# A state-space layer between two expert layers: a two-phase convolution for the first batch, and a router with wide products between its narrow ones

## The chip, the cores and the metric

The kernel is one program on one core of a Trainium2 chip. The core has a matrix engine (TensorE, PE in the rows; its weight loads are PEld), VectorE (DVE), ScalarE (ACT), GpSimd (POOL) and SyncE (SP), which here only issues transfers. The engines run side by side and wait for one another on semaphores. The metric is the device time of one execution in microseconds (us). Three runs of the kernel before took 1475.5, 1475.68 and 1467.76 us, median 1475.5.

## The reference

The input x has 8 batches of 512 tokens of 256 numbers. Four layers follow one another, each added to x after a layer norm of its input:

```
x = x + attention(layernorm(x))      # linear attention, 16 heads
x = x + experts(layernorm(x))        # softmax router, best of 8 experts, 256 -> 512 -> 256
x = x + state_space(layernorm(x))    # below
x = x + experts(layernorm(x))        # the same weights again
```

The state-space layer projects each token to 512 channels, runs a full convolution over 4 successive tokens (512 channels in, 512 out) and adds a bias; call the result u. From u come the step dt = clip(sigmoid(u W + b)), and two vectors B and C of 16 numbers for every token. Then for each of 512 channels and 16 states a linear recurrence runs over the 512 tokens, `state = exp(dt * A) * state + dt * B * u + 1e-6`, and y is the sum of the states times C, plus D * u; y is gated by silu(z) and projected back to 256. Everything is float32.

## The kernel before, in words

All of x stays on the chip (32 tiles of 128 tokens). The stages are written one after another, each engine's program in an order written out by hand; no planner orders anything.

**Attention** (0 to about 196 us) and, grown into its end, the **first router**. `x_turn` (L1300 through `turned`) transposes a batch of x, ScalarE copies it, and `logits` (L1419) multiplies it with the router's weights, which are only 8 columns wide. VectorE then computes the routing in one chain of small steps (`feed`, L999 to L1059). TensorE helps it twice: with two products by a triangle and by ones (L1464, L1466), and with four groups of 8 products of 80 columns (L1475) that turn the places of the tokens into lists. VectorE prepares the next group while TensorE works on the last. The semaphore `f_lg` lets the first pair start, `f_hot` each group.

**The folded taps.** Projection and convolution are both linear, so the kernel multiplies them first: 4 taps times 2 halves give 8 products, each of four 128x512 matmuls (`tap`, L1449), copied by ScalarE to `tapw` (`tap_copy`, L618). Their inputs are `ipw` (the projection) and `cw` (one tap of the convolution, 1 MB), which SyncE loads at L369 and L373 after the rows of x and their scales have been stored. Products 0 to 3 of the eight are made during the first router, as work for TensorE between the steps of the chain; products 4 to 7 follow the expert layer.

**The expert layer** (239 to 393 us) gathers 39 tiles of tokens in the order of their experts and is bound by TensorE (L1504, L1513). Its result goes to memory and comes back into x by 8 loads (L382).

**The first batch of the state-space layer** (407 to 472 us) is prepared in the open, since no recurrence runs yet. VectorE takes the statistics of the layer norm (L839, for tiles 4 to 31 in one piece, then its scales). ScalarE normalises (`m_norm`, L686), TensorE transposes (`m_turn`), ScalarE copies (`m_xtcopy`, L693). `m_conv` (L1567) makes each 128 channels of u (four outputs `o`) with 8 matmuls of 512 columns: 4 taps times 2 halves of the input. ScalarE adds the bias (`m_uevac`, L699). `m_uturn` (L1575) turns u, `m_bcmm` (L1584) gives B and C, `m_dtmm` (L1598) the input of dt, again four outputs of four matmuls. ScalarE takes tanh (`m_thevac`, L718), VectorE clips (`m_clip`, L1121), TensorE turns dt (`m_dturn`, L1613), VectorE multiplies dt and u (`m_weigh`, L1134), and ScalarE multiplies by B for the first state (`m_input`, L755, four tiles). `m_spread` (L1300) turns that product into PSUM, and the first recurrence (`m_scan`, L1197) can run. ScalarE has also to make the exponentials (`m_decay`, L745) and to normalise batch 1.

**The loop** (472 to about 1260 us) has 64 slots for each of 8 batches, one recurrence in each. In every slot ScalarE makes one exponential and one tile of input, TensorE turns one tile and does the preparation of the next batch by a table of slots (`CONV_AT` and so on), GpSimd multiplies by C. The router and the expert layer of the end follow (to 1469 us); there TensorE has products by ones between its groups (`spin`, L1455), whose result nobody reads.

## Time and profile before

| | |
|---|---|
| three runs | 1475.5, 1475.68, 1467.76 us |
| the profiled execution | 1471.08 us, its span 1469.3 us |
| busy: TensorE, VectorE, ScalarE, GpSimd | 1366.5, 1011.8, 937.7, 861.1 us |
| mean granted TensorE clock | 0.978 |
| the chain that ended last | TensorE 67%, ScalarE 16%, VectorE 10% |

The span runs from the first instruction to the last; 1.8 us of the execution lie around it. The chain of waits goes back from the last instruction to whatever released each step, so it tells which engine a stretch waits for. Granted clock is 1.00 for 2.4 GHz and 0.50 for 1.2 GHz. TensorE does a float32 product in two passes, each with a record of its own: "x16" of L1567 in the rows is 8 matmuls of the code. A transpose has one record.

### The profile page before, as it was taken

Reading aid. Unit: us, or ns where it says so; the run is one execution under the profiler, and the core shown is the slowest. Engines: PE = TensorE matmul, PEld = TensorE weight load, DVE = VectorE, ACT = ScalarE, POOL = GpSimd, SP = SyncE. Lnnn points to the kernel's source line nnn. Section 1 sums busy time; section 2 is a strip of 40 time slices with the busy share of each in tenths; the row PEclk is TensorE's granted clock in tenths of the full one; section 3 lists DMA queues with packets and bytes.
Section 4 is the critical chain, followed back from the end, with each engine's and each line's share of the span. In section 5 each row is a group of like instructions: output and inputs, shape, how many; then the busy total and the mean of one; then the engine's idle time right before and its main releaser. Section 6 shows DMA issues by size and latency. Waiting matters only on the chain.

```text
span 1469.3 us, 22230 instructions
## 1 busy us (share of the span) xinstructions
PE 1366.5 (93%) x7040; PEld 949.6 (65%) x7040; DVE 1011.8 (69%) x1529; ACT 937.7 (64%) x1737; POOL 861.1 (59%) x436
## 2 busy tenths in 40 slices
PE   5899998999998999999999999999999887979997
PEld 2566686999744555565655655655656576569996
DVE  6666634333332899899899898998998988853332
ACT  1222231344314999899999998999999999214442
POOL 1111002555200899798898897998988979225552
PEclk9999989999998999999999999999999979999999
DMA  9200044777420598898997997988979979376662
GB/s 301 85 29 29 19 98 144 211 206 210 153 65 16 118 219 195 179 221 186 201 222 181 205 220 176 218 190 193 223 170 204 230 195 234 79 235 203 208 210 82
DMA packets 108229, 248.39 MB, mean 169 GB/s; under 512 B 19097, under 2 KB 49950, under 8 KB 94048
## 3 DMA queue, kind: packets, MB, share of 16 engines
q0 software_dynamic: 23104, 131.96, 41.5%
q1 hardware_dynamic: 82944, 113.68, 25.6%
q10 hardware_dynamic: 2080, 1.47, 0.3%
q8 instruction: 55, 0.90, 0.2%
q14 instruction: 46, 0.38, 0.1%
HBM read 116.72 MB, written 18.94 MB: 92 GB/s over the span
## 4 chain that ended last, share of the span: by engine, by line
PE 67%; ACT 16%; DVE 10%; issue 4%; DMA 1%; another core or an unknown queue 1%; SPq 0%; DVEq 0%; ACTq 0%; POOLq 0%; POOL 0%
PE ps L1300 11%; PE ps L1513 9%; PE ps L1504 9%; PE ps L1567 7%; ACT arena L745 7%; PE ps L1598 7%; ACT arena L755 7%; PE ps L1325 4%; PE ps L1640 3%; PE ps L1629 3%; DVE arena L1197 3%; PE ps L1362 2%; PE ps L1584 2%; PE ps L1316 2%; PE ps L1449 1%
## 5 line engine op out<-in xcount | busy, mean ns | idle before, releaser
L500 POOL TENSOR_TENSOR arena<-arena 128x2048 f32<-128x2048 f32 x91 | 425.1, 4684 | 118.6 <-DVE arena L1197 117.4
L1300 PEld LDWEIGHTS ps<-cst,arena 128*128 128x128 f32 x2428 | 295.3, 143 | 280.1 <-issue 187.7
L1197 DVE TENSOR_TENSOR_SCAN arena<-arena,ps 128x512 f32<-128x512 f32 x364 | 431.7, 1209 | 62.3 <-PE ps L1300 58.7
L1300 PE MATMUL ps<-cst,arena 128*128 128x128 f32 x2428 | 365.7, 278 | 51.2 <-ACT arena L755 24.3
L745 ACT ACTIVATE arena<-arena,a_neg 128x512 f32<-128x512 f32 x512 | 365.9, 715 | 43.3 <-DVE arena L1197 29.6
L755 ACT ACTIVATE arena<-arena,m_bt 128x512 f32<-128x512 f32 x512 | 362.9, 709 | 3.8 <-DVE arena L1134 2.2
L1567 PE MATMUL ps<-arena,tapw 128*128 128x512 f32 x512 | 255.1, 600 | 0.7 <-ACT arena L693 0.7
L1197 DVE TENSOR_TENSOR_SCAN x<-arena,ps 128x512 f32<-128x512 f32 x148 | 175.7, 1209 | 21.9 <-PE ps L1300 20.6
L500 POOL TENSOR_TENSOR x<-x,arena 128x2048 f32<-128x2048 f32 x36 | 169.8, 4728 | 14.7 <-DVE x L1197 12.7
L1078 DVE TENSOR_TENSOR arena<-ps,arena 128x256 f32<-128x256 f32 x78 | 33.1, 425 | 205.7 <-PE ps L1513 131.4
L456 POOL DMA_INDIRECT arena<-rows,arena x78 | 75.9, 973 | 158.1 <-DVE arena L1058 134.9
L1504 PEld LDWEIGHTS ps<-arena 128*128 128x128 f32 x1248 | 154.7, 196 | 3.8
L1504 PE MATMUL ps<-arena 128*128 128x128 f32 x1248 | 154.9, 279 | 0.0
L1513 PE MATMUL ps<-arena 128*128 x624 | 147.5, 380 | 3.3 <-ACT arena L644 3.3
L637 ACT ACTIVATE arena<-ps 128x256 f32<-128x256 f32 x78 | 30.0, 385 | 157.8 <-PE ps L1300 156.5
L1598 PE MATMUL ps<-arena,dtw 128*128 128x512 f32 x256 | 128.6, 597 | 0.6 <-ACT arena L699 0.6
L1513 PEld LDWEIGHTS ps<-arena 128*128 128x128 f32 x624 | 112.5, 190 | 16.0 <-issue 3.7
L644 ACT ACTIVATE arena<-ps,b1t 128x128 f32<-128x128 f32 x312 | 89.3, 370 | 43.8 <-issue 29.5
L1567 PEld LDWEIGHTS ps<-arena,tapw 128*128 128x128 f32 x512 | 85.1, 193 | 36.1 <-issue 33.7
L447 POOL TENSOR_TENSOR x<-x,arena 128x1024 f32 (+1 forms) x8 | 18.9, 2358 | 120.0 <-DVE arena L868 114.4
L471 POOL DMA_INDIRECT residual<-arena x39 | 39.4, 1011 | 68.4 <-DVE arena L1085 67.2
L471 POOL DMA_INDIRECT out_x<-arena x39 | 39.3, 1008 | 67.5 <-DVE arena L1085 67.5
(164 smaller groups left out, 1573.0 us busy)
## 6 DMA issues: line engine op xcount, KB each, us to landing
arena<-arena POOLq DMA_DIRECT2D x52, 1024.0 KB, 8.3
arena<-in_W SPq DMA_DIRECT2D x94, 512.0 KB, 8.2
arena<-c_rows SPq DMA_DIRECT2D x128, 256.0 KB, 3.7
arena<-x POOLq DMA_DIRECT2D x28, 1024.0 KB, 8.4
x<-arena POOLq DMA_DIRECT2D x24, 1024.0 KB, 8.3
rows<-x SPq DMA_DIRECT2D x16, 512.0 KB, 4.2
x<-residual SPq DMA_DIRECT2D x12, 512.0 KB, 5.9
x<-in_x SPq DMA_DIRECT2D x8, 512.0 KB, 11.2
```

The source lines that it names most:

```text
L456: g.indirect_dma_start(out=t_x[j % XB], out_offset=None, in_=xs[r], in_offset=bass.IndirectOffsetOnAxis(ap=idx[:, j:j + 1], axis=0))\
L471: g.indirect_dma_start(out=x_mid if r == 0 else T["out"].rearrange("b s d -> (b s) d"), out_offset=bass.IndirectOffsetOnAxis(ap=idx[:, j:j ...
L500: g.tensor_tensor(h, h, m_c[i % RC].unsqueeze(1).to_broadcast([P, KI, SEQ]), ALU.mult)\
L644: last = a.activation(t_ht[par][:, k, :], ps[4 + par][:, k * P:(k + 1) * P], ACT.Relu, bias=b1t[:, row(e), k:k + 1].rearrange("p a b -> p ...
L745: a.activation(m_a[g % RA], m_dt[b % 2][:, k, :], ACT.Exp, scale=a_neg[:, k, n:n + 1])\
L755: a.activation(m_dbt[i % 2][:, c, :], m_wt[b % 2][:, c, :], ACT.Copy, bias=1e-6, scale=m_bt[b % 2][:, c, n:n + 1]).then_inc(S("m_dbt"), 1)
L1197: v.tensor_tensor_scan(out=h[:, k, :], data0=m_a[g % RA], data1=ps[SCAN_BANK[g % 3]][:, :], initial=0.0, op0=ALU.mult, op1=ALU.add).then_i ...
L1300: return t.transpose(bank, src[:, k * P:(k + 1) * P], ident)
L1504: last = t.matmul(ps[4 + par][:, h * P:(h + 1) * P], t_w1[j % WR][:, k, h * P:(h + 1) * P], t_xt[par][:, k, :], start=(k == 0), stop=(k == ...
L1513: last = t.matmul(ps[6 + par][:, 0:D], t_ht[par][:, k, :], w2[:, row(e), k, :].rearrange("p a h -> p (a h)"), start=(k == 0), stop=(k == K ...
L1567: mm = t.matmul(ps[CONV_BANK[o]][:, :], tapw[:, k, d, o * P:(o + 1) * P], m_xt[n % 2][:, d, k:k + SEQ], start=(i == 0), stop=(i == TAPS * ...
L1598: mm = t.matmul(dt_bank(n, o)[:, :], dtw[:, k, o * P:(o + 1) * P], m_u[n % 2][:, k, :], start=(k == 0), stop=(k == KI - 1))
```

## The change

In the **router**: SyncE loads `ipw` and the first two taps at the start of the program, behind the other weights, and not after the stores. The four matmuls of product 0 are made one by one in rounds 3 to 6 of the loop over `x_turn` and `logits`; product 1 takes the place that product 0 had, product 2 that of products 1 and 2, and the four matmuls of product 3 stand one behind each group of L1475. Other banks hold the results.

In the **first batch**: u is split into odd and even tokens. With a0 to a3 the taps and x the input, both phases share the sums (a3 + a2) and (a1 + a0) times the even tokens of x, 4 matmuls of 256 columns (`both_bank`). Each phase then adds 4 matmuls of 256 (or 255) columns by single taps and differences of neighbouring tokens. GpSimd makes the two sums of taps (`tap_sum`, 1024 elements a lane each) and the two differences (`xd_first`, 512 elements a lane each). ScalarE copies the shared part with the bias into the odd places of u (`m_both`), and VectorE adds it to both phases (`m_join`), which takes the place of `m_uevac`. VectorE's statistics are cut so that each join falls between two pieces. In the **last steps** `m_dturn` of output 1 goes between the matmuls of output 3, those of 2 and 3 to both sides of the first half of batch 1's transposes; VectorE clips before it weighs; ScalarE normalises batch 1 earlier and makes only two of the four tiles of the first input, VectorE the other two. The other batches are as before. Some semaphores are shared by both routers (`f_n`, `f_yb`).

```diff
@@ -32,6 +32,9 @@
 PAD = TAPS - 1
+HALF = SEQ // 2
+TURN_OF = ((0, 0), (0, 1), (1, 1), (1, 0))
+PARTS, BOTH_END = 3 * len(TURN_OF), len(TURN_OF) - 1
 LN_EPS, NORM_EPS = 1e-5, 1e-6
...
@@ -85,6 +88,9 @@
+TAP_BANK = (7, 1, 0, 1, 0, 1, 0, 1)
...
@@ -269,6 +276,12 @@
                 for c in (RING * CPB, (RING + 2) * CPB)]
+        def first_h(j):
+            return m_h[j].rearrange("p k t -> p (k t)")
+        xd_first = first_h(0)[:, 0:2 * KD * HALF].rearrange("p (s k t) -> p s k t", s=2, k=KD)
+        tap_sum = first_h(1).rearrange("p (j k n) -> p j k n", j=2, k=KD)
         m_c = [s.take(SEQ) for _ in range(RC)]
...
@@ -335,6 +354,15 @@
+            def send_tap(k):
+                if k >= 2:
+                    sp.wait_ge(S("tap_mm"), KD * (k - 1))
+                sp.dma_start(cw[k % 2], T["conv"][k].rearrange("(k p) d -> p k d", p=P)).then_inc(S(f"ld_cw{k}"), 16)
+            sp.dma_start(ipw, T["ip_x"].rearrange("(k p) d -> p k d", p=P)).then_inc(S("ld_cw0"), 16)
+            send_tap(0)
+            send_tap(1)
@@ -366,14 +394,7 @@
             sp.wait_ge(S("row_zeroed"), 32)
-            sp.dma_start(ipw, T["ip_x"].rearrange("(k p) d -> p k d", p=P)).then_inc(S("ld_cw0"), 16)
-            def send_tap(k):
-                if k >= 2:
-                    sp.wait_ge(S("tap_mm"), KD * (k - 1))
-                sp.dma_start(cw[k % 2], T["conv"][k].rearrange("(k p) d -> p k d", p=P)).then_inc(S(f"ld_cw{k}"), 16)
-            for k in range(TAPS - 1):
-                send_tap(k)
+            send_tap(2)
             send_w1(0)
@@ -481,6 +502,15 @@
+            for j in (1, 0):
+                g.wait_ge(S("tapw"), KD * (TAPS - 2 * j))
+                g.tensor_tensor(tap_sum[:, j], tapw[:, TAPS - 1 - 2 * j], tapw[:, TAPS - 2 - 2 * j], ALU.add)\
+                    .then_inc(S("m_zero"), 1)
+            g.wait_ge(S("m_xtc"), KD)
+            for s in range(2):
+                g.tensor_tensor(xd_first[:, s], m_xt[0][:, :, PAD + 1 - 2 * s:PAD + SEQ - 2 * s:2],
+                                m_xt[0][:, :, PAD:PAD + SEQ - 1:2], ALU.subtract).then_inc(S("m_xd"), 1)
@@ -615,7 +645,7 @@
                 a.wait_ge(S("tap_mm"), n + 1)
-                a.activation(tapw[:, n // KD, n % KD, :], ps[n % 2][:, :], ACT.Copy).then_inc(S("tapw"), 1)
+                a.activation(tapw[:, n // KD, n % KD, :], ps[TAP_BANK[n]][:, :], ACT.Copy).then_inc(S("tapw"), 1)
@@ -699,6 +729,12 @@
+            def m_both(o):
+                a.wait_ge(S("m_bothmm"), o + 1)
+                a.activation(m_u[0][:, o, 1::2], both_bank[:, o % 2 * HALF:(o % 2 + 1) * HALF], ACT.Identity,
+                             bias=mvec[:, 0, o:o + 1]).then_inc(S("m_both"), 1)
@@ -778,22 +814,22 @@
                     m_utevac(0, o - 1)
-                m_uevac(0, o)
+                m_both(o)
             m_utevac(0, KI - 1)
             m_bchi(0)
-            for o in range(KI):
+            for o in range(KI - 1):
                 m_thevac(0, o)
-                if o == 2:
-                    for k in range(KD):
-                        m_decay(k)
+            for k in range(KD):
+                m_decay(k)
+            for c in range(XN):
+                m_norm(1, c)
+            m_thevac(0, KI - 1)
             for g in range(KD, AHEAD):
                 m_decay(g)
-            for c in range(XN):
-                m_norm(1, c)
-            for c in range(CPB):
-                m_input(0, c)
             for c in range(XN, CPB):
                 m_norm(1, c)
+            for c in range(CPB // 2):
+                m_input(0, c)
             for k in range(KD):
...
@@ -1103,18 +1139,26 @@
             v.wait_ge(S("ld_mid0"), 16)
-            def m_stats(lo, hi):
-                first_stats(lo, hi)
+            def shifts(lo, hi):
                 v.scalar_tensor_tensor(out=nw[2][:, lo:hi], in0=mean[:, lo:hi], scalar=-1.0, in1=rstd[:, lo:hi],
...
-            m_stats(0, CPB)
+            first_stats(0, CPB)
+            shifts(0, CPB)
...
+            def m_join(o):
+                v.wait_ge(S("m_both"), o + 1)
+                v.wait_ge(S("m_umm"), o + 1)
+                u = m_u[0][:, o, :].rearrange("p (t s) -> p t s", s=2)
+                v.tensor_tensor(u, ps[CONV_BANK[o]][:, :].rearrange("p (s t) -> p t s", s=2),
+                                u[:, :, 1].unsqueeze(2).to_broadcast([P, HALF, 2]), ALU.add).then_inc(S("m_u"), 1)
@@ -1264,9 +1308,31 @@
             v.wait_ge(S("ld_mid1"), 16 * (BATCH - 1))
-            m_stats(CPB, NCH)
-            for q in range(SLOTS):
-                m_pre(0, q)
+            for c in range(CPB, NCH // 2):
+                row_stats(c)
+            m_join(0)
+            for c in range(NCH // 2, NCH - 1):
+                row_stats(c)
+            link(row_stats(NCH - 1))
+            m_join(1)
+            layer_norm_scales(CPB, NCH)
+            shifts(CPB, NCH)
+            m_join(2)
+            m_join(3)
+            m_clip(0, 0)
+            m_clip(0, 1)
+            m_btcopy(0)
+            m_weigh(0, 0)
+            m_clip(0, 2)
+            m_weigh(0, 1)
+            m_weigh(0, 2)
+            m_clip(0, 3)
+            m_weigh(0, 3)
+            v.wait_ge(S("m_wt"), KI)
+            v.wait_ge(S("m_btc"), 1)
+            for c in range(CPB // 2, CPB):
+                v.tensor_scalar(m_dbt[0][:, c, :], m_wt[0][:, c, :], m_bt[0][:, c, 0:1], 1e-6, ALU.mult, ALU.add)\
+                    .then_inc(S("m_dbt0"), 1)
             binds = v.value_load(far_flag[0:1, 0:1], min_val=0, max_val=P * KI * NS)
@@ -1420,6 +1486,19 @@
+            def tap_part(n, c):
+                k, d = n // KD, n % KD
+                if c == 0:
+                    t.wait_ge(S(f"ld_cw{k}"), 16 if k else 32)
+                    if n == 0:
+                        t.wait_ge(S("a_xadd"), BATCH)
+                    if n >= 2:
+                        t.wait_ge(S("tapw"), n - 1)
+                mm = t.matmul(ps[TAP_BANK[n]][:, :], ipw[:, c, d * P:(d + 1) * P], cw[k % 2][:, c, :],
+                              start=(c == 0), stop=(c == KI - 1))
+                if c == KI - 1:
+                    mm.then_inc(S("tap_mm"), 1)
@@ -1438,17 +1517,13 @@
-            def tap(k, d):
-                t.wait_ge(S(f"ld_cw{k}"), 16 if k else 32)
-                n = KD * k + d
-                if n >= 2:
-                    t.wait_ge(S("tapw"), n - 1)
+                if 0 <= i - 3 < KI:
+                    tap_part(0, i - 3)
+            def tap(n):
                 for c in range(KI):
-                    last = t.matmul(ps[n % 2][:, :], ipw[:, c, d * P:(d + 1) * P], cw[k % 2][:, c, :],
-                                    start=(c == 0), stop=(c == KI - 1))
-                last.then_inc(S("tap_mm"), 1)
+                    tap_part(n, c)
@@ -1459,14 +1534,13 @@
                     t.wait_ge(S("f_raw"), BATCH - 1)
-                    tap(0, 0)
+                    tap(1)
                 t.wait_ge(S("f_lg"), 2 * r + 2)
...
                 if r == 0:
-                    for n in range(1, 3):
-                        tap(n // KD, n % KD)
+                    tap(2)
                 else:
@@ -1476,14 +1550,15 @@
                     last.then_inc(S("f_inv"), 1)
-                    if r and i < NCH // GROUP - 1:
+                    if r == 0:
+                        tap_part(3, i)
+                    elif i < NCH // GROUP - 1:
                         spin(1)
                 if r == 0:
-                    tap(1, 1)
                     t.wait_ge(S("tapw"), KD * 2)
                 def tr(par, n):
-                    t.wait_ge(S(f"f{r}_n{par}"), n + 1)
+                    t.wait_ge(S(f"f_n{par}"), tiles_done(r, par) + n + 1)
                     if not (isinstance(n, int) and n == 0):
...
@@ -1552,6 +1627,32 @@
+            def m_conv_first(o, i):
+                part, (d, j) = i // len(TURN_OF), TURN_OF[i % len(TURN_OF)]
+                first, last = i % len(TURN_OF) == 0, (i + 1) % len(TURN_OF) == 0
+                if o == 0 and i == 0:
+                    t.wait_ge(S("m_zero"), 4)
+                    t.wait_ge(S("m_xtc"), KD)
+                if o == 0 and part and first:
+                    t.wait_ge(S("m_xd"), part)
+                if o and i == 0:
+                    t.wait_ge(S("m_both"), o)
+                if o >= 2 and part == 1 and first:
+                    t.wait_ge(S("m_utc"), o - 1)
+                if part == 0:
+                    lo = o % 2 * HALF
+                    mm = t.matmul(both_bank[:, lo:lo + HALF], tap_sum[:, j, d, o * P:(o + 1) * P],
+                                  m_xt[0][:, d, PAD - 2 * j:PAD - 2 * j + SEQ - 1:2], start=first, stop=last)
+                else:
+                    lo = (2 - part) * HALF
+                    mm = t.matmul(ps[CONV_BANK[o]][:, lo + j:lo + HALF], tapw[:, TAPS - part - 2 * j, d, o * P:(o + 1) * P],
+                                  xd_first[:, part - 1, d, 0:HALF - j], start=first, stop=last)
+                if i == BOTH_END:
+                    mm.then_inc(S("m_bothmm"), 1)
+                if i == PARTS - 1:
+                    mm.then_inc(S("m_umm"), 1)
@@ -1646,7 +1747,9 @@
                 if k == 0:
-                    t.wait_ge(S("m_dbt"), g + CPB)
+                    t.wait_ge(S("m_dbt"), g + CPB - CPB // 2)
+                if g == 0:
+                    t.wait_ge(S("m_dbt0"), CPB // 2)
                 if g >= 3:
...
@@ -1723,9 +1826,9 @@
             for o in range(KI):
-                for i in range(TAPS * KD):
-                    m_conv(0, o, i)
-                    if o and i == TAPS:
+                for i in range(PARTS):
+                    m_conv_first(o, i)
+                    if o and i == PARTS // 2:
                         m_uturn(0, o - 1)
@@ -1741,9 +1844,13 @@
                 m_dtmm(0, 3, k)
-            for o in range(1, KI):
-                m_dturn(0, o)
-            for c in range(CPB):
+                if k == 1:
+                    m_dturn(0, 1)
+            m_dturn(0, 2)
+            for c in range(XN):
+                m_turn(1, c)
+            m_dturn(0, 3)
+            for c in range(XN, CPB):
                 m_turn(1, c)
```

## Rows read from the trace of the kernel before

**Rows 1.** Chain of waits, first router (start us, length us, what).

```profile
204.27 10.97 DMA arena<-in_conv
215.38 5.73 PE ps L1449 x8
```

**Rows 2.** Timeline of TensorE, first router (start, length, what, idle before).

```profile
205.37 1.85 PE L1419 MATMUL ps<-wr,arena 128*128 128x8 f32 x16
...
207.98 5.64 PE L1419 MATMUL ps<-wr,arena 128*128 128x8 f32 x32
```

**Rows 3.** Busy TensorE, weight loads, VectorE, ScalarE, GpSimd; granted clock, DMA share, GB/s: first router.

```profile
207.00:209.00 2.00, 2.00 (x20) 2.00 (x21) 0.00 (x0) 1.01 (x3) 0.00 (x0) 1.00 0.80 98
209.00:219.00 10.00, 8.25 (x29) 6.12 (x29) 4.07 (x10) 1.08 (x4) 0.00 (x0) 0.51 0.72 232
```

**Rows 4.** Timeline of VectorE, first router.

```profile
213.99 0.42 DVE L999 TENSOR_TENSOR arena<-arena,scales 128x256 f32<-128x256 f32 x1 [12.34 <-ACT arena L599]
...
217.07 0.60 DVE L1008 TENSOR_TENSOR arena<-arena 128x256 f32<-128x256 f32 x1
...
221.65 0.42 DVE L1016 TENSOR_REDUCE arena<-ps 128x8 f32<-128x256 f32 x1 [3.35 <-PE ps L1464]
...
237.62 0.20 DVE L1057 TENSOR_SCALAR arena<-ps 128x40 f32<-128x40 f32 x1 [0.96 <-PE ps L1475]
```

**Rows 5.** Timeline of VectorE, second router.

```profile
1286.71 0.59 DVE L1008 TENSOR_TENSOR arena<-arena 128x256 f32<-128x256 f32 x1
...
1288.16 0.42 DVE L1016 TENSOR_REDUCE arena<-ps 128x8 f32<-128x256 f32 x1 [0.23 <-PE ps L1464]
...
1304.77 0.20 DVE L1057 TENSOR_SCALAR arena<-ps 128x40 f32<-128x40 f32 x1 [1.66 <-PE ps L1475]
```

**Rows 6.** Timeline of SyncE's queue, 0 to 70 us.

```profile
38.84 0.43 SPq L336 DMA_DIRECT2D mvec<-in_mvec  x1
63.70 0.38 SPq L341 DMA_DIRECT2D rows<-x  x1
```

**Rows 7.** Chain of waits, first batch of the state-space layer.

```profile
410.96 12.96 PE ps L1567 x26
...
425.34 7.07 PE ps L1567 x16
...
442.30 2.77 PE ps L1567 x6
...
457.93 3.44 PE ps L1598 x8
...
463.19 0.67 PE ps L1613 x4
...
466.35 0.70 DVE arena L1134
...
467.08 2.56 ACT arena L755 x4
...
470.18 2.03 PE ps L1300 x8
```

**Rows 8.** Chain of waits, expert layer: 256 columns moving.

```profile
255.71 1.73 PE ps L1513 x8
```

**Rows 9.** Groups of VectorE in 195 to 260 us, shapes apart.

```profile
L1031 DVE TENSOR_REDUCE arena<-arena 128x32 f32<-128x256 f32 x1 | 0.6, 604 | 0.0
L1001 DVE TENSOR_REDUCE arena<-arena 128x32 f32<-128x256 f32 x1 | 0.4, 420 | 0.0
```

**Rows 10.** Groups of GpSimd, shapes apart.

```profile
L447 POOL TENSOR_TENSOR x<-x,arena 128x1024 f32 x7 | 16.5, 2356 | 114.4 <-DVE arena L868 114.4
```

**Rows 11.** Timeline of VectorE, first batch.

```profile
411.70 9.24 DVE L839 BATCH_NORM_STATS2 stats<-x 128x6 f32<-128x256 f32 x28 [3.40 <-DMA x<-residual]
```

**Rows 12.** Busy time by stretches, first batch, with granted clock (columns as in rows 3).

```profile
411.00:414.00 3.00, 3.00 (x4) 1.44 (x5) 2.29 (x7) 0.40 (x1) 0.00 (x0) 0.50 0.01 3
...
466.00:475.00 9.00, 5.99 (x21) 4.01 (x20) 1.91 (x2) 7.14 (x13) 0.00 (x0) 0.50 0.01 2
```

20 lines of the change are left out of this document (12 added, 8 removed).

## The prediction, made before the changed kernel was run

> **What bounds the kernel now.** I read the chain of waits first, then the timelines of each engine in the two stretches that the change touches, then the granted clock there. Everything between these stretches (attention, both expert layers, the loop of 64 slots a batch) is left alone by the diff, so its length should stay and only its start should move.
>
> In the first router the chain goes through a transfer and then through VectorE. SyncE begins to load the first tap at 204.27, behind the rows and the scales; it lands 10.97 us later and product 0 starts at 215.38 [rows 1]. Its four wide matmuls take 5.73 us there, because TensorE runs at 1.2 GHz: the granted clock is 1.00 to 209 and 0.51 from 209 to 219 [rows 3]. The second product by ones stands behind product 0, so VectorE, which had the one-hot table ready at 217.67, gets on only at 221.65 and has waited 3.35 us [rows 4]. From there VectorE needs 15.97 us to the list of tokens (L1057, 237.62), and the expert layer can start.
>
> In the first batch the chain is TensorE almost throughout: 16 records of 512 columns take 7.07 us, 0.442 each [rows 7]. The convolution ends at 445.07 (442.30 + 2.77); call that E. The matmuls of dt's last output start at E + 12.86 and take 3.44. Then comes a stretch in which each step waits for another engine: turns at 463.19, the last weighing at 466.35, four inputs by ScalarE from 467.08 (2.56 us), eight transposes from 470.18 that take 2.03 us at half clock; the first recurrence can start at 472.21, E + 27.14 [rows 7]. The clock is 0.50 from 466 to 475 [rows 12].
>
> **Convolution.** Removed: 4 outputs x 8 matmuls x 2 records x 0.442 = 28.3 us. Added: 4 x 12 x 2 records of 256 columns. The nearest row is the expert layer's product of 256 columns, 8 records in 1.73 us, 0.216 each [rows 8]: 20.8 us. That is -7.5. The unknown is the moving operand with a step of two in the shared part (16 of the 48 matmuls, 6.9 us); no row of TensorE shows one. VectorE reads with a step 0.604 us for what takes 0.420 without, 1.44 times [rows 9]; at that price the shared part costs 3.0 more. Below nothing is excluded, since the same columns pass. I take nothing, because the step is of two elements here and of 32 there, and keep +3.0 for the range. The Trainium skill (SBUF: State Buffer, Door 1: The DMA port swizzle) says that a line of 16 bytes with two hits is read at full rate; a step of two has two hits, so by it the term is nothing, and by the row +3.0.
>
> The start: GpSimd's first sum can run before the last tap is copied, the second takes 2.36 us [rows 10] from 407.7 and ends near 410.1, or 410.7 if it stands behind the first. TensorE has waited until 410.96 for the first copy of x and now waits for both copies: +0.5. The differences have half the elements, 1.2 us each, and are wanted 1.7 and 3.5 us later (at 2.4 GHz; later still at 1.2): hidden, and at twice the price 1.3 us would show. VectorE has 9.24 us of statistics from 411.70 [rows 11]; 12 tiles end at 415.7, join 0 is due near 418, the other 16 tiles need 5.3 us and end near 424, join 1 is due near 424.6, the scales (3.5 us) end near 429 and join 2 is due near 431. Each join (0.7, as the weighing [rows 7]) is wanted by the turn 7 matmuls or 3 us later, so a join a third slower for its steps still costs nothing. The copy of the shared part has the same cover. If the statistics came late, the turn would wait for the join. Half clock at the start: 411 to 414 costs 1.5 us now [rows 12] and should again. Sum: -7.0.
>
> **Last steps**, from the new E with all parts at full clock. Output 3 of dt: 12.86 + 3.44, and a turn of 0.45 between: 16.75. Turn of output 2: 17.2; weighing it: 17.9; clip 3 (tanh was ready at 17.5): 18.6; turn 3 (0.67): 19.3; weighing (0.70): 20.0; two inputs on ScalarE (half of 2.56): 21.3, while VectorE makes the other two, 1.2 to 1.4 together if they are as long as a pass from PSUM; four transposes (0.45): 21.8. Half of batch 1's transposes fall into the wait for clip 3, the rest behind turn 3, ending before 21.3. Against 27.14 that is -5.3. ScalarE's two normalisings moved ahead of tanh 3 use 1.1 us in which it would wait for TensorE; the new single queue order leaves tanh 3 free at 15.1, due at 16.75. At half clock the transposes take 0.85: -4.9.
>
> **Clock behind it.** Between 472.2 and 475.5 TensorE still runs at half clock on matmuls of batch 1, which are the chain: 1.6 us. The stretch without wide matmuls shrinks from 10.8 us (461.4 to 472.2) to 5.1. Between -1.6 and 0 I take -0.8.
>
> **Router.** The early loads (2.5 MB) follow at 39.3, and the queue is empty until 63.7 [rows 6]: nothing waits. Four wide matmuls now lie between the narrow products: +3.5 us on TensorE. If they keep the clock up, the last 32 narrow records take 3.4 instead of 5.64 (16 take 1.71 at full clock [rows 2]); the logits end 1.2 later and L999 runs at 215.2, not 213.99. The table is ready at 218.9; product 1 has ended at 218.3; in the second router L1016 follows 0.86 after the end of L1008 [rows 5], so it runs at 219.8, -1.9. Then the four groups with one wide matmul between: the second router has that pattern, 16.61 us from L1016 to L1057 against 15.97 [rows 4, 5], +0.6. Together L1057 at 236.4: -1.2. What was product 3 behind the groups (3.65 us) lay under the gathering and gives nothing. Product 2 alone ends near 223.3, the first group is due at 226.4: 3 us of idle TensorE that can cost the clock and up to 1.5 us. The term lies between -1.9 and +2.4 (below); I take -1.2.
>
> **Sum:** -7.0 - 5.3 - 0.8 - 1.2 = -14.3, against the profiled 1471.08: 1456.8. That execution lies 4.4 under the median of the three runs; the four have a mean of 1472.5, and 14.3 under that is 1458. I give **1458**.
>
> **Rivals.**
> 1. *The clock falls where I keep it.* A stretch of narrow products or transposes alone has cost it twice [rows 3, 12]. If the logits end at half clock, they end 2 us later still and product 1 takes 3.5 more, partly in the wait for the table: L1057 1.2 to 2.4 later than now. In the last steps half clock costs 0.4 and the 0.8 behind. Sum -10: 1462. For it: the wide matmuls stop at round 6, and the last 3.4 us before product 1 are narrow as before. Against: narrow products had run since attention's end near 196 before the clock fell at 209, while the wide ones now come every 3.5 us to 210.5; and the wait without them in the last steps is halved.
> 2. *The strided operand costs 1.44 times:* 3.0 less gain, 1461. For it only VectorE's row.
> 3. *The lead is partly eaten in the loop.* If ScalarE, not TensorE, sets the first slots, the clock's part and some of the ordering are lost: gain near 7, 1465. Against: ScalarE's start moves up by the same 5 us, as its inputs and copies hang on the same weighing.
> 4. *Slower: half-width matmuls, with a weight load for each 256 columns, don't lift the clock from 1.2 GHz after the wait at 407.* The convolution then takes 41.5, +20.8, and if it goes on through the 32 records of dt (+14) and B and C (+4), 38 us in all: 1495. It decides at a third of that stretch at half clock: there the gain is gone. Against: the expert layer runs nothing wider than 256 columns, 0.216 each, which is the full clock.
>
> **Chances.** My forecast 0.5 (1453 to 1461 by the bounds), rival 1 0.25, rival 2 0.08, rival 3 0.08, rival 4 0.04, an unforeseen rest 0.05. The range 1449 to 1467 holds the first three and most of the fourth; its upper end adds 3.5 us for the spread of the runs, which differ by 8 us without a change. One per cent is 14.8 us, about what a measurement of this kernel can tell from no change, and my gain stands at that border: against the median of 1475.5, 1458 is 1.2% less, against the profile 1.0%. So faster by over 1% gets four fifths of the forecast and two fifths of rivals 1 and 2 (where the median before stays high), 0.40 + 0.13, say 0.52; slower by over 1% is rival 4, 0.04; within 1% the rest, 0.44.
>
> **What would show it.** In the chain after: 96 records of 256 columns in 20.8 us at clock 1.00; the distance from the last of them to the first recurrence near 21.8, not 27.1; L1016 near 219.8 and L1057 near 236.4; clock 1.00 from 197 to 226; ScalarE's wait for the weighing before L755's successor shorter by 5. A shared part longer than the other two parts of an output shows rival 2, a turn of u waiting for a join shows a missing cover, clock 0.50 beyond the first 3 us of the convolution shows rival 4. I am wrong if the loop's length from the first recurrence changes by more than 2 us.

## The result, and the profile after

Timed against the kernel before on the same chip, the changed kernel took 1464.92 us (median of 13 runs, 1460.01 to 1480.33) where before took 1475.5 (13 runs): ratio 0.995, 95% interval 0.9928 to 0.9972, so 4 to 11 us less. A second set of 12 runs gave 1466.43 and a ratio of 0.9963 (0.9941 to 0.9985). I had forecast 1458 and a gain of 14.3 us. The time lies in the range; the gain, 7 us by the first ratio and 6 by the mean spans, is half of what I said or less. The mean span, which I use below to compare kernels since it has the smallest error, is 1464.6 us over 25 runs, and 1470.1 to 1471.0 for before in the five later sets: **-6, with a standard error of 1**. Every "+-" below is such a standard error. The profiled execution took 1464.08 us (span 1462.3).

The first router after, by its chain of waits (start, length, what). It answers to [rows 1, 2, 4]:

```profile
207.42 0.96 PE ps L1497 x2
...
210.95 0.96 PE ps L1497 x2
211.91 0.87 PE ps L1366 x8
212.78 3.47 PE ps L1485 x32
216.25 5.24 PE ps L1497 x8
221.49 0.45 PE ps L1539 x2
```

And busy time by stretches, with the clock behind the five engines (answers to [rows 3]):

```profile
209.00:217.00 8.00, 8.00 (x63) 7.05 (x62) 0.38 (x1) 2.76 (x7) 0.00 (x0) 1.00 0.01 2
217.00:221.00 4.00, 4.00 (x7) 1.64 (x6) 3.69 (x10) 0.90 (x2) 0.00 (x0) 0.57 0.00 0
```

The 32 narrow products now run at full clock (3.47, was 5.64), but the clock falls behind them, and product 1 takes 5.24 us. VectorE, on its timeline, has the table ready at 220.3 and waits again:

```profile
219.70 0.60 DVE L1044 TENSOR_TENSOR arena<-arena 128x256 f32<-128x256 f32 x1
...
222.03 0.42 DVE L1052 TENSOR_REDUCE arena<-ps 128x8 f32<-128x256 f32 x1 [1.10 <-PE ps L1539]
...
238.65 0.20 DVE L1093 TENSOR_SCALAR arena<-ps 128x40 f32<-128x40 f32 x1 [1.66 <-PE ps L1549]
```

L1052 is L1016 of before and L1093 is L1057. The wait ends at 222.03, not at 219.8 as I had it, and the lists come at 238.65, where before had 237.62.

The first batch after, by the chain (answers to [rows 7]):

```profile
410.35 3.75 PE ps L1646 x8
414.11 4.04 PE ps L1650 x16
418.15 1.81 PE ps L1646 x8
419.96 1.29 PE ps L1650 x6
421.25 0.44 PE ps L1676 x4
421.69 0.97 PE ps L1685 x2
422.66 2.35 PE ps L1650 x10
...
438.75 5.15 PE ps L1699 x12
...
456.57 0.69 DVE arena L1165
...
457.31 0.67 PE ps L1714 x4
...
458.00 0.70 DVE arena L1178
...
458.73 1.34 ACT arena L791 x2
...
460.11 1.12 PE ps L1366 x4
461.23 1.71 PE ps L1668 x2
```

L1646 is the shared part with a step of two, L1650 the two parts on differences. E is 438.75 (445.07 before). The input for the first recurrence is ready at 461.23, E + 22.5. The recurrence itself starts later, at 462.50, E + 23.7:

```profile
462.50 3.51 DVE L1241 TENSOR_TENSOR_SCAN arena<-arena,ps 128x512 f32<-128x512 f32 x3 [2.89 <-ACT arena L781]
```

The bracket names ScalarE's exponential, but that had ended at 461.64. VectorE comes from a branch (the test of `binds`): the branch instruction, L1337, ends at 459.44, and the first instruction inside the branch, a wait at L1236, stands at 462.43. Between these two lie 2.8 to 3.1 us in all 20 traces. With the old last steps they are over 2.1 to 2.4 us ahead of the first recurrence, which then waits for its input; in every kernel with the new ones the recurrence starts within 0.1 us behind them.

The clock in both places (answers to [rows 12]):

```profile
408.00:415.50 7.50, 6.18 (x17) 4.54 (x18) 4.02 (x12) 1.92 (x4) 3.08 (x3) 0.54 0.21 67
415.50:459.00 43.50, 41.95 (x169) 26.73 (x167) 16.89 (x48) 10.88 (x20) 0.00 (x0) 1.00 0.05 13
459.50:463.00 3.50, 2.89 (x8) 1.75 (x9) 0.61 (x2) 3.50 (x7) 0.00 (x0) 0.51 0.03 7
```

GpSimd's sums and differences, and VectorE's statistics with the first two joins (answers to [rows 10, 11]), on the timelines:

```profile
404.39 4.65 POOL L507 TENSOR_TENSOR arena<-tapw 128x1024 f32<-128x1024 f32 x2
410.29 2.04 POOL L511 TENSOR_TENSOR arena<-arena 128x512 f32<-128x512 f32 x2 [1.25 <-ACT arena L723]
```

```profile
410.18 4.02 DVE L875 BATCH_NORM_STATS2 stats<-x 128x6 f32<-128x256 f32 x12 [3.31 <-DMA x<-residual]
418.25 0.69 DVE L1160 TENSOR_TENSOR arena<-ps,arena 128x512 f32<-128x512 f32 x1 [4.05 <-PE ps L1650]
418.86 5.31 DVE L875 BATCH_NORM_STATS2 stats<-x 128x6 f32<-128x256 f32 x16
425.15 0.69 DVE L1160 TENSOR_TENSOR arena<-ps,arena 128x512 f32<-128x512 f32 x1 [0.98 <-PE ps L1650]
```

All of it is hidden: no turn of u waits for a join.

Then the part that I had taken as fixed. Seven batches take 685.3 us from the fifth recurrence of the first batch to the first recurrence of the last, in all 20 traces within 0.1. But the last batch, the exit of the loop and the second router's first steps differ. TensorE's waits from 35 to 60 us after the last batch's first recurrence, in the second trace of the changed kernel (engine, line, what it waited for, us, times, longest):

```profile
PE ps L1366 <- DMA arena<-rows: 6.9, 1, 6.9
PE ps L1366 <- ACT arena L791: 2.5, 3, 1.2
```

and in the kernel before:

```profile
PE ps L1300 <- ACT arena L755: 3.3, 3, 1.3
```

SyncE brings back four batches of rows there for the second router, into buffers that have just come free. The fourth load is issued 36.6 us into the batch in every trace with the old order of these loads, but for one experiment (conv_only, 37.5). Its line in the list of DMA issues (KB, us from issue to landing) is, before:

```profile
arena<-rows SPq DMA_DIRECT2D x1, 512.0 KB, 11.1
```

and in the two traces of the change:

```profile
arena<-rows SPq DMA_DIRECT2D x1, 512.0 KB, 16.2
```

```profile
arena<-rows SPq DMA_DIRECT2D x1, 512.0 KB, 21.1
```

TensorE is to turn these rows at slot 34 and stands until they are there. Behind it, in the profile after, VectorE stands at the exit of its branch (chain of waits):

```profile
1253.85 0.05 DVE x L1248
...
1254.00 2.39 issue
1256.39 1.89 DVE x L1248 x3
```

In the trace of before this issue takes 0.44 us.

### The profile page after: what moved, and what is told of

It is laid out like the page before. It is cut to its first block, busy times and chain, and to the rows that moved or that the text cites. A ratio compares the mean times of both kernels' runs of the same rounds, so it can differ in the third digit from the quotient of the medians.

```text
span 1462.3 us, 22311 instructions
## 1 busy us (share of the span) xinstructions
PE 1363.0 (93%) x7072; PEld 959.2 (66%) x7072; DVE 1017.6 (70%) x1535; ACT 934.8 (64%) x1735; POOL 868.0 (59%) x440
## 4 chain that ended last, share of the span: by engine, by line
PE 68%; ACT 17%; DVE 9%; issue 4%; DMA 2%; POOL 0%; DVEq 0%; POOLq 0%; ACTq 0%; SPq 0%
PE ps L1366 11%; PE ps L1579 10%; PE ps L1588 9%; ACT arena L781 7%; PE ps L1699 7%; ACT arena L791 7%; PE ps L1668 5%; PE ps L1391 4%; PE ps L1741 3%; PE ps L1730 3%; DVE arena L1241 2%; PE ps L1428 2%; PE ps L1685 2%; PE ps L1382 2%; PE ps L1497 2%
## 5 line engine op out<-in xcount | busy, mean ns | idle before, releaser
L1366 PEld LDWEIGHTS ps<-cst,arena 128*128 128x128 f32 x2428 | 299.7, 145 | 279.3 <-issue 190.9
L1366 PE MATMUL ps<-cst,arena 128*128 128x128 f32 x2428 | 370.4, 281 | 50.3 <-ACT arena L791 23.8
L781 ACT ACTIVATE arena<-arena,a_neg 128x512 f32<-128x512 f32 x512 | 366.1, 715 | 40.7 <-DVE arena L1241 30.0
L1668 PE MATMUL ps<-arena,tapw 128*128 128x512 f32 x448 | 224.5, 595 | 0.0
L667 ACT ACTIVATE arena<-ps 128x256 f32<-128x256 f32 x78 | 29.9, 383 | 159.4 <-PE ps L1366 159.4
L674 ACT ACTIVATE arena<-ps,b1t 128x128 f32<-128x128 f32 x312 | 89.0, 368 | 41.3 <-issue 31.8
L1668 PEld LDWEIGHTS ps<-arena,tapw 128*128 128x128 f32 x448 | 72.5, 191 | 18.0 <-issue 16.8
```

Source lines behind the costliest of these rows:

```text
L674: last = a.activation(t_ht[par][:, k, :], ps[4 + par][:, k * P:(k + 1) * P], ACT.Relu, bias=b1t[:, row(e), k:k + 1].rearrange("p a b -> p ...
L781: a.activation(m_a[g % RA], m_dt[b % 2][:, k, :], ACT.Exp, scale=a_neg[:, k, n:n + 1])\
L1366: return t.transpose(bank, src[:, k * P:(k + 1) * P], ident)
L1668: mm = t.matmul(ps[CONV_BANK[o]][:, :], tapw[:, k, d, o * P:(o + 1) * P], m_xt[n % 2][:, d, k:k + SEQ], start=(i == 0), stop=(i == TAPS * ...
```

## The experiments

Eighteen runs followed, of fifteen kernels, before and the change among them. The table holds every trace that has been taken. **Router** is from attention's last addition to the lists; **conv** from the start of the last copy of the taps to the start of the convolution's last record, some 0.4 us ahead of E; **steps** from there to the start of the fifth recurrence; **end** from the last batch's first recurrence to the second router's reduction of the product by ones (L1016, L1052); **load** the moment in the last batch at which the fourth load of rows lands; **code** the moments of TensorE's program loads there between 10 and 60 us (below). All in us.

| kernel | router | conv | steps | end | load | code | span |
|---|---|---|---|---|---|---|---|
| before | 40.9 | 37.4 | 35.6 | 122.8 | 47.7 | 29, 56 | 1469.3 |
| before, again | 47.8 | 35.9 | 35.3 | 122.6 | 47.8 | 30, 52 | 1470.9 |
| before, third trace | 42.8 | 37.6 | 35.6 | 122.9 | 47.9 | 30, 56 | 1466.2 |
| before, fourth trace | 46.5 | 38.8 | 34.3 | 127.2 | 52.7 | 30, 52 | 1475.0 |
| router_only | 42.6 | 38.8 | 34.3 | 127.2 | 52.8 | 30, 53 | 1473.4 |
| steps_only | 41.2 | 38.8 | 30.4 | 123.8 | 47.9 | 30, 56 | 1462.3 |
| conv_long | 42.8 | 34.1 | 34.0 | 123.5 | 47.6 | 29, 53 | 1465.3 |
| after_long | 42.6 | 30.2 | 28.6 | 123.2 | 47.8 | 30, 56 | 1456.7 |
| after_long_again | 44.3 | 32.8 | 29.9 | 122.2 | 47.5 | 29, 55 | 1463.3 |
| before_long | 41.3 | 35.9 | 35.6 | 124.4 | 49.0 | 18, 46 | 1465.8 |
| after | 40.9 | 32.7 | 29.9 | 128.6 | 52.7 | 18, 45 | 1462.3 |
| after, again | 42.6 | 32.8 | 29.9 | 133.5 | 57.6 | 18, 45 | 1466.5 |
| batch_only | 47.7 | 31.8 | 28.7 | 128.0 | 50.4 | 18, 46 | 1466.0 |
| conv_only | 46.5 | 32.8 | 33.8 | 129.6 | 52.5 | 20, 47 | 1470.7 |
| conv_warm | 55.8 | 31.9 | 30.2 | 129.1 | 50.5 | 18, 46 | 1475.9 |
| back_early | 42.6 | 32.8 | 30.0 | 122.2 | 40.8 | 18, 45 | 1457.2 |
| batch_back | 47.8 | 31.8 | 28.6 | 122.9 | 40.5 | 18, 45 | 1458.9 |
| before_back | 43.0 | 35.9 | 35.3 | 122.6 | 45.1 | 33, 53 | 1465.2 |
| before_long_back | 46.5 | 38.8 | 34.3 | 122.8 | 40.7 | 18, 45 | 1471.2 |
| after_long_back | 42.6 | 30.2 | 28.6 | 127.5 | 42.4 | 33, 55 | 1462.0 |

(The first trace of before is [rows 1 to 12].) One trace is one draw; the timed runs decide, and each set follows with its ratio to before.

**The two kernels again.** No edit.

> The kernel before, unchanged, a second execution in the profile. Theory A (what the changed kernel lost behind the first batch is chance of single executions: where the clock falls in the last batch, and waits for code at jumps): the time from the 5th recurrence (480.1 in the first profile) to the 512th (1261.8), 781.7 us there, moves by 2 us or more, and the 5 us that ScalarE waits for its first relu in both expert layers may be 3. Theory B (they are fixed by the program): 781.7 within 0.5 and both waits near 5 us. Time ratio to the kernel before 1.000 in both.

> The changed kernel, unchanged, a second execution in the profile. Theory A: the gain up to the 5th recurrence stays near -11.9 with the expert layer's wait, -9 to -10 without; the half clock in the last batch (24 us in the first profile behind 1176, against 17 before) and the 2.39 us of VectorE behind the loop change. Theory B: both come back within 0.5 us. Ratio 0.993 to 0.997 in both.

Before against itself: ratio 1.0002 (0.9978 to 1.0027). After: 0.9963 (0.9941 to 0.9985). From the fifth recurrence to the last, before took 781.7 and 781.6 us in its two traces, the change 784.2 and 790.1: there each execution of the changed kernel drew its own length. The stall of ScalarE at the first expert layer (5.8 us of waiting), which made the first trace of before some 2.5 us longer, was not in the second (2.0). The first router took 47.8 us there, not 40.9: the trace on which I had priced the router was a lucky one.

**Parts of the change.** router_only has the early loads, the wide products between the narrow ones, their banks, and the old first batch; batch_only the reverse. conv_only and steps_only divide batch_only:

```
# conv_only: m_conv_first, m_join, tap_sum, xd_first, m_both; behind E the old order
# steps_only: the old m_conv(0, o, i); behind E the new order, half of the inputs on VectorE
```

> Only the router's part of the change: early loads, wide products between narrow ones; the first batch as before. Theory A (my term of -1.2 was too good, since the clock falls after the last 32 narrow products and product 1 runs at half clock): the start of the four groups to L1057 as before, 54.6 us from attention's last batch, ratio 0.999 to 1.001. Rival (the whole gain was the router's, with the stall of the expert layer gone for good): L1588's first record 2.5 us earlier against attention, ratio 0.998.

> Only the first batch's part of the change, the router as before (product 0 behind the late load). Theory A: from the last folded tap's copy to the end of the convolution 33 us, not 38; from there to the first recurrence's input 22.5, not 27.1; together with the clock behind it -10.4 at the 5th recurrence; ratio 0.993. Rival (the lead is given back later in the loop): the 5th recurrence -10, the 512th -7 or less, ratio 0.996.

> Only the convolution of the first batch in two phases (GpSimd's sums and differences, the joins on VectorE); the old order of the last steps and the old router. Theory A (the two-phase convolution is worth what the profile of the full change shows: 96 records of 256 columns for 128 halves of 512, a start about half a microsecond later, 2.4 us lost to half clock instead of 1.5): the stretch from the last copy of the taps to E 32 to 33 us, not 36 to 37; total about -5 us. Theory B (a part of this gain is taken back after E, since the joins load VectorE and the old order of the last steps waits for it): E earlier by 5, but E to the first recurrence longer than 27.8; total -2 to -3. Theory C (the end of the loop takes 4 us or more from whatever kernel starts it earlier): total within 1 us of before, the last batch longer than 98 us.

> Only the new order of the last steps before the first recurrence; the old convolution and the old router. Theory A: E to TensorE's first spread 22.5 us instead of 27.1, first to fifth recurrence 5 instead of 7.8, total -5 to -7 us. Theory B (the order gains only because the new convolution leaves VectorE free or finishes the statistics earlier): E to first recurrence no shorter than 26 us, total -1 to -2. Theory C (given back in the last batch): stage gain as in A, total within 1 us of before. The two halves together should give the -7.7 us (mean span) of the kernel with only the first-batch part; if they add to clearly more, they share a gain.

router_only: 1.0004 (0.998 to 1.0028), mean span +0.9 +-1.4. batch_only: 0.9958 (0.9938 to 0.9978), -7.7 +-1.2, the ratio that its rival had. conv_only: 0.9995 (0.9979 to 1.0012), -1.1 +-1.1, where its trace shows 5 us gained in the convolution: theory C. steps_only: 0.9984 (0.9967 to 1.0001), -3.7 +-1.2, where its trace shows 5: nearer to A. The two add up to -4.9 +-1.7, against the -7.7 of both together, which the errors allow. The halves share no gain in the traces: 37.5 to 32.0 in the convolution and, behind it, 35.0 (with the old convolution) to 29.5 are the means of the table's old and new forms (without conv_long). The convolution's half loses its gain outside the batch.

**Rows brought back earlier.**

```
-BACK_AT = (1, 2, 5, 6)
+BACK_AT = (1, 2, 4, 5)
```

> The full change, and in the last batch SyncE issues the third and fourth load of staged rows one recurrence group earlier (at 24.4 and 29.8 us after the start of the last batch, was 29.8 and 36.6). Theory A (what gives back the gain at the end is that the fourth of these loads lands 16 to 21 us after its issue and TensorE's turn of those rows at slot 34 waits for it, 0.8 to 6.9 us): no wait there, last batch 96.4 us instead of 98.8 and 104.8, total 2 to 5 us less than the full change. Theory B (some of the 16 DMA engines fall behind in that stretch anyway, and the accumulations and rows of C behind them are what counts): the wait moves to the rows of C or to the final sums, the last batch stays at 98 to 105 us and the total is that of the full change. Theory C (longer last batches are chance of single executions): total as the full change, last batch anywhere from 96 to 105.

0.9935 (0.9911 to 0.9959), mean span 1461.3 +-1.8: 3.3 +-2.0 less than the change. TensorE's wait for rows is gone, the load lands at 40.8 and the end is back at 122.2. Theory A, as far as this goes.

**TensorE kept busy before the convolution.**

```
+            hold(1)       # matmuls of 512 columns by ones, result unread
             t.wait_ge(S("weights"), 2)
...
+            hold(3)
             for o in range(KI):
```

> The full change with four matmuls of 512 columns by ones, whose result nobody reads, in TensorE's idle time before the convolution (one ahead of the wait for the weights' sum, three between the turns of x and the first product). Theory A (TensorE's clock is half at 408.4 to 415.2 because it has been idle or turning since 405.6, and costs 2.4 us of the convolution): clock 1.00 there, the stretch from the last copy of the taps to E 30.5 instead of 32.7, total -2 against the full change. Theory B (the clock falls anyway, as it did in the kernel with a busy TensorE at the first router): the same half clock, the stretch 32.7 or up to 0.5 longer because the added matmuls at half clock push the first product. Before any of it: the added matmuls take 1.7 us of 2.2 us idle at full clock.

0.9954 (0.9931 to 0.9977), mean span 1465.8 +-1.8: no gain. The clock was 1.00 there as A had it, but conv fell only from 32.7 to 31.9, as the added matmuls push the first product. In its trace the first router ran for 34.1 us at half clock, so that one span says nothing.

**Is the longer end the kernel's or the execution's?**

> The kernel before once more, for its trace. Seven traces of kernels with a part of the change took 123.9 to 133.5 us from the start of the last batch to the second router's product by ones (mean 128.6), two of the kernel before 122.6 and 122.8. Theory A (the end takes longer because of the change): this one again 122.5 to 123.5. Theory B (each execution draws its own length there, by the clock, the DMA engines and the exit of the loop's branch, whatever the kernel): as likely as not above 124. First router: 24.9 and 30.5 so far; anywhere between 24 and 39.

> The same as the look before: theory A 122.5 to 123.5 us from the start of the last batch to the second router's product by ones, theory B as likely as not above 124.

> The kernel before, with only the third and fourth load of staged rows issued one group earlier in the last batch. Theory A (these loads matter only to kernels with the change, whose DMA engines fall behind there): no change, within 1.5 us of before. Theory B (they cost any kernel some executions): 2 to 4 us less than before, as much as the same edit gave on the full change (3 to 4 us, medians 1460.6 against 1464.9 and 1466.4).

> Only the first-batch part (two-phase convolution and the new order), the old router, and the earlier loads of staged rows. Theory A (parts add up: first-batch part -7.8, earlier loads -3.5, router part nothing): mean span near 1459.5, that is -11, ratio near 0.9925. Theory B (the router part is worth its 1.2 us or more): slower than the full change with the earlier loads (1461.3), 1462 to 1464. Theory C (the gain of the earlier loads was chance): as the first-batch part alone, 1463.

The two further traces of before took 122.9 and 127.2: chance has a part (B). But three of four traces of before lie at 122.6 to 122.9, and up to here no kernel with the new convolution and the old loads of rows is under 128.0. before_back: 0.9993 (0.9972 to 1.0014), mean 1469.1, -1.6 +-1.2, between the bounds of A and B and not decided. batch_back: 0.9944 (0.9921 to 0.9966), mean 1461.9, as fast as back_early, which has the router part too, but only 1.0 +-1.3 under batch_only, where A had 3.5.

**The place of the program loads.** The DMA view has queue 8 with kind "instruction", packets of 16 KB. In the whole trace of before there are 55, for 15122 instructions of TensorE, so one for some 275. The traces of the change have 67 instructions more, 64 of them by the 16 matmuls that the new convolution adds (two weight loads and two products each). Of the kernels so far, only those with the new convolution have these packets near 18 and 46 us of the last batch. From 44 to 48 us of the last batch, before (queue, kind, packets, MB, share):

```profile
q0 software_dynamic: 89, 0.60, 71.9%
q1 hardware_dynamic: 363, 0.47, 33.3%
q14 instruction: 1, 0.01, 0.5%
```

and, in the same stretch after, the line that before lacks:

```profile
q8 instruction: 1, 0.02, 1.5%
```

That is the stretch in which the rows land. Three kernels move these loads by waits that are already fulfilled, placed where TensorE is mostly idle, and change nothing else. Two such waits make one instruction: 67 more in before_long, 188 more in the other two, which with the change's 67 is about the distance from one packet to the next:

```
+            def lengthen(n):
+                for _ in range(n):
+                    t.wait_ge(S("ld_cst"), 16)
```

> The kernel before with 67 more instructions in TensorE's program, waits that are already fulfilled, in its idle time before batch 0's transposes and before batch 0's product of keys and values in attention; as many as the two-phase convolution adds there. Theory A (what gives the gain back at the end is the place of TensorE's program loads: packets of 16 KB, at 29, 56, 74 and 95 us of the last batch in the old convolution's kernels and at 18, 45, 70 and 95 in the new one's): the loads move to 18, 45, 70 and 95, the stretch from the start of the last batch to the second router's product by ones takes 127 to 130 us instead of 122.8 (three traces of four), and the mean span is 2 to 5 us more than before, 1473 to 1476. Theory B (the loads' place is a mark of the new convolution, not the cause): loads move, the stretch stays at 122.8, mean span 1470 to 1472. Theory C (the program's length doesn't move the loads): they stay at 29, 56, 74.

> The kernel with only the two-phase convolution, and 188 more waits that are already fulfilled in TensorE's program, in idle time in attention, behind the first router and before the convolution: with the 65 instructions of the convolution 253, nearly one packet of 256. Theory A: the program loads are back at 29, 56, 74 and 95 us of the last batch, the end stretch at 122.8 instead of 129.6, and the gain of 5 us in the first batch shows in the total: mean span 1465 to 1467, 3 to 5 less than the 1469.9 without the waits. Theory B: the end stretch stays near 129 or is drawn anew, mean span 1469 to 1471.

> The full change with 188 more fulfilled waits in TensorE's program (with the 67 of the change 255). Theory A: loads at 29, 56, 74 and 95 us of the last batch, end stretch 122.8 (one in four 127), mean span 1460 to 1462 instead of 1464.4 and 1464.9, as the earlier loads of staged rows gave (1461.3). Theory B: mean span 1464 to 1466, end stretch 127 to 134 as in the two traces of the full change.

The loads went where theory A of each had them. before_long: 1.0035 (1.0015 to 1.0056), mean span 1474.9 +-1.2, **+4.4**; the profiled run was the shortest of the twelve (1465.8, next 1471.0), so its end of 124.4 is no measure of them, and no trace shows where the 4.4 go. In the stretch from 44 to 48 us it now has a load of code too:

```profile
q8 instruction: 1, 0.02, 1.5%
```

conv_long: 0.999 (0.997 to 1.001), 1469.0 +-1.1, only 0.9 +-1.5 under conv_only: by the time, B. Its waits cost something of their own: TensorE's first transposes start at 14.4 us (12.3 in the profile after), conv is 34.1 where conv_only has 32.8. With these 2.1 and 1.3 back the gain would be some 4, an estimate. after_long: 0.9929 (0.9901 to 0.9957), six runs.

> The kernel before with the 67 fulfilled waits in TensorE's program and the third and fourth load of staged rows issued one group earlier. Theory A (the moved program loads cost 4.4 us through the late landing of the staged rows): the earlier loads take it away, mean span 1469 to 1471.5, rows landed by 45 us, end stretch 122.5 to 124.5. Theory B (they cost it elsewhere, in TensorE's clock at the first router, in the exit of the branch or the second router): mean span stays 1473 to 1476, and the trace shows the time there.

> The full change with the 188 fulfilled waits once more, since only six of its runs count so far (mean span 1459.8). If the place of the program loads matters: 1459 to 1462, 3 to 5 less than the full change (1464.4 and 1464.9). If the six were luck: 1463 to 1466. The trace should have the end stretch at 122.8 to 124.5 us (was 123.3).

> The full change with both: 188 fulfilled waits and the earlier loads of staged rows. Theory A (both remove the same wait for the staged rows): as with either alone, mean span 1459.5 to 1462. Theory B (they remove different things): 1456 to 1459.

before_long_back: 1.0011 (0.999 to 1.0032), 1470.6 +-0.6: 4.3 us are gone once the rows come early (A). after_long_again: 0.9944 (0.9922 to 0.9966), 1461.1; with the six, 1460.7 over 18 runs, 3.9 +-1.1 under the change, or some 6, an estimate, without the 2.1 that the waits cost. after_long_back: 0.9956 (0.9937 to 0.9976), 1462.4: no more than either alone (A). The mean spans side by side, with errors of 0.6 to 1.8:

| mean span | as it is | code loads moved | rows early | both |
|---|---|---|---|---|
| before | 1470.1 to 1471.0 | 1474.9 | 1469.1 | 1470.6 |
| the change | 1464.6 | 1460.7 | 1461.3 | 1462.4 |

## Why the prediction was wrong, point by point

**The step that failed** is the sentence that everything outside the two stretches keeps its length. I had named it as the test (the loop may not change by more than 2 us): from first recurrence to last it is 789.5 us before, 789.9 and 796.0 in the two traces after, where the first five recurrences alone are 2 us shorter. The batch's gain is there: 37.5 to 32.0 and 35.0 to 29.5, 11.0 in all where my terms for it were 13.1. The router's 1.2 is not. The end takes back 5: 128.9 us is the mean of the six traces with the loads of code near 18 and 46 us and the rows at their old place, 123.9 that of the nine with them near 30 and 53, 123.6 that of the five with the rows early. 11 less 5 is the 6 measured. Moved on purpose, the same loads cost the kernel before 4.4 us.

The timed runs show that the place of the code loads costs time: 4.4 +-1.4 us when before gets it, 3.9 +-1.1 when the change loses it. They show for before that the earlier loads of rows remove the cost, which ties it to these rows, since the padding moves the code loads of every other stage as well. With the change the evidence for the rows is weaker (3.3 +-2.0, and 1.0 +-1.3 in batch_only). By what wait it costs differs from trace to trace. TensorE waits for the rows only in four: 0.8 and 6.9 us with the change, 3.0 in router_only, 2.9 in the fourth trace of before. In others a row of C is late instead. GpSimd's waits 35 to 60 us into the last batch, in conv_only and in batch_only:

```profile
POOL arena L525 <- DMA arena<-c_rows: 7.7, 1, 7.7
```

```profile
POOL arena L525 <- DMA arena<-c_rows: 5.9, 1, 5.9
```

and in the first trace of before:

```profile
POOL arena L500 <- DMA arena<-c_rows: 0.8, 1, 0.8
```

But such a wait alone is no proof of a longer end: steps_only has one of 3.6 us with an end of 123.8, before_back one of 3.1 with 122.6.

Four things stay open. How a load of code delays the rows: the fourth trace of before and router_only had them late with the code loads in their old place, so the new place makes it likely and is not its only cause. What makes the branch's exit stall (0 to 3.7 us more; in batch_only and conv_warm, with the half clock behind it, that is the whole excess; after_long_back has 2.8 with the rows early, and conv_long 1.3 with the code loads in their old place). Why batch_only gained only 1.0 by the earlier rows where the full change gained 3.3. And what the clock adds: over the end stretch the mean granted clock is 0.93 in the first trace of before, 0.85 in both of the change, 0.90 in back_early, and no run separates whether the lower clock is a cause or follows from the waits.

**Convolution, -7.0 predicted, -5.5 in the means, -4.7 from trace to trace.** The mechanism was right and the terms were mis-sized. An output takes 1.81 + 1.29 + 2.35 = 5.45 us against 7.07, so 6.5 saved, not 7.5: 0.227 us a record, where [rows 8] gave 0.216. Start: 4.7 us behind the last copy, was 3.9; GpSimd's sums (2.3 each, the second ending at 409.0) are ready before the second copy of x, and it is this copy that TensorE waits for. Half clock costs 2.3 us here (8 records in 3.75 for 1.81, 16 in 4.04 for 3.64), not 1.5; in after_long and after_long_back the clock was full and conv 30.2. How much of this stretch runs at half clock is drawn anew in each execution, with either kernel, so the fairer comparison is at equal mean granted clock: 35.9 against 30.2 at 1.00, 37.4 against 31.8 near 0.95, 38.8 against 32.8 near 0.91. That is 5.6 to 6.0 us, where the two first traces (0.96 and 0.90) give 4.7.

**Strided operand, rival 2:** refuted. The shared part takes 0.226 us a record, the others 0.228. The Trainium skill (SBUF: State Buffer, Door 1: The DMA port swizzle) has a line of 16 bytes with two hits read at full rate, and a step of two has two; the trace agrees.

**Last steps and the clock behind, -6.1 predicted, -5.5 in the means:** near in the sum, off in both parts. From E to the first recurrence I had 27.1 to 21.8, and it is 23.7. The input is ready at E + 22.5, since the spread at half clock took 1.12 for 0.45, as rival 1 had it. The other 1.3 us are VectorE's branch, 3.0 us from its instruction to the next, which my sum did not have, as the old order hid it. With the new last steps it decides when the first recurrence starts, in after_long too, where the clock was full. From the first to the fifth recurrence 2.1 us were gained (7.5 to 5.5 in the means), and I had 0.8. That the two errors nearly cancel is luck.

**Router, -1.2 predicted:** nothing that can be measured (+0.9 +-1.4 alone). Rival 1 held: product 1 came at half clock again, 5.24 us. My price for the wait removed came from one trace; the stretch drew 40.9 to 47.8 us in twelve traces with the old router and 40.9 to 55.8 in eight with the new. In seven of those eight 3 to 10 us of it are at half clock, in the twelve 10 to 27: the wide products seem to hold the clock as meant, but the timed runs show no gain by it.

**Rival 3** (lead eaten in the first slots) is refuted by the 685.3 us of the seven batches. **Rival 4** is refuted: from 415.5 on the clock is 1.00. No rival of mine had the last batch.

## What to carry to other kernels

Added instructions in one stage of a kernel written out in full move its program loads in all later ones: price the margin of each late transfer (here 2 to 4 us between landing, 47.7, and use, 50 to 52) before taking the rest as fixed, and give it more when a buffer's last reader allows. Where a part's trace gain and its timed gain differ, look at the stages that it does not touch. Price a wait from several traces if the clock has a hand in it: the first router of the unchanged kernel drew 40.9 to 47.8 us. And when a stretch is shortened, list what it hid: here a branch of 3 us on VectorE.

The earlier loads of rows are the version to keep: with the change they gave the best ratio that needs no padding, 0.9935, though its interval (0.9911 to 0.9959) overlaps that of the change alone.

## What the runs showed beside this

- Fulfilled waits that do nothing made the kernel before 4.4 +-1.4 us slower and the change 3.9 +-1.1 us faster. One load of 16 KB comes for some 275 instructions of TensorE.
- VectorE's branch ahead of the loop takes 2.8 to 3.1 us from the branch instruction to the next one, in all 20 traces.
- A run's span follows its mean granted clock: in the five sets of before (23 to 35 runs) the correlation is -0.59 to -0.86, and 0.001 of clock goes with 0.6 to 1.2 us of span.
- The trace that happened to be first decided two of my terms (the router's wait, ScalarE's stall of 2.5 us); four traces of the same kernel had spans from 1466.2 to 1475.0.
